# Attention with the keys on the partitions, and three norms centred inside one accumulation group

## The reference

```python
x = _layernorm(x + _L0_attn_ref(x, ...))   # two mamba directions, norms, a small MLP
x = _layernorm(x + _L0_ffn_ref(x, ...))    # gated FFN, hidden 512, two gelu layers
x = _layernorm(x + _L1_attn_ref(x, ...))   # 8 heads, 2 key heads, causal
x = _layernorm(x + _L1_ffn_ref(x, ...))    # 8 experts, top 2
```

```python
k_lat = (x @ wk_down)   # 2 key heads of 32 latent channels
v_lat = (x @ wv_down)
scores = einsum('bqhrd,bkhd->bhrqk', q, k) * scale, causal mask
probs = softmax(scores, axis=-1)
y = einsum('bhrqk,bkhd->bqhrd', probs, v) @ wo
```

## Time and profile before

| | |
|---|---|
| time, 3 runs | 2446.17 us median (2445.69 to 2449.73) |
| the profiled execution | 2451.41 us |
| its span, first to last instruction | 2449.6 us |
| mean granted TensorE clock | 0.863 |

### The profile page before, as it was taken

How to read it: one execution, slowest core, us unless ns; L and a number is a source line. 1 busy time by engine, 2 the same in 40 slices (tenths; PEclk the granted TensorE clock), 3 DMA queues, 4 the chain that set the end, 5 groups by cost and what they waited for, 6 DMA issues and landing times.

```text
span 2449.6 us, 28585 instructions
## 1 busy us (share of the span) xinstructions
PE 1828.0 (75%) x7192; PEld 829.5 (34%) x7192; DVE 1663.3 (68%) x2756; ACT 1221.4 (50%) x2140; POOL 956.7 (39%) x870
## 2 busy tenths in 40 slices
PE   5424976788768887788777887688867788667788
PEld 2201333343324333343333433343333433333344
DVE  2996478845789378873788557884687927887143
ACT  3333655546445465536555365554644456553252
POOL 0453146422455035450464324642354604544031
PEclk9556988899889997799887998889977999889998
DMA  7984465606555274543756156560755536453000
GB/s 200 222 218 112 106 161 146 168 14 177 135 145 134 62 175 130 134 100 86 172 146 146 45 132 154 133 171 25 183 134 129 130 78 163 130 144 75 0 1 5
DMA packets 102732, 301.56 MB, mean 123 GB/s; under 512 B 15216, under 2 KB 31232, under 8 KB 102528
## 3 DMA queue, kind: packets, MB, share of 16 engines
q1 hardware_dynamic: 98304, 297.20, 48.5%
q10 hardware_dynamic: 4224, 2.10, 0.3%
HBM read 280.39 MB, written 18.87 MB: 122 GB/s over the span
## 4 chain that ended last, share of the span: by engine, by line
issue 43%; PE 24%; DVE 17%; POOL 10%; ACT 4%; DVEq 1%; POOLq 0%; SPq 0%; DMA 0%; ACTq 0%
PE ps_g L626 10%; DVE sb_hst L1107 7%; POOL sb_hc L1322 6%; PE ps_g L703 3%; DVE ps_in L1100 3%; POOL sb_h L1336 2%; PE ps_g L711 2%; PE ps_att L626 2%; PE ps_y L579 2%; PE ps_att L723 2%; DVE sb_nmax L1218 1%; POOL sb_res L1348 1%; ACT sb_mix L948 1%; POOL sb_dd L1312 1%; DVE sb_h L1268 1%
## 5 line engine op out<-in xcount | busy, mean ns | idle before, releaser
L1322 POOL TENSOR_TENSOR sb_hc<-sb_hst,sb_crep 128x512 f32<-128x512 f32 x512 | 652.5, 1275 | 637.9 <-DVE sb_hst L1107 637.9
L1107 DVE TENSOR_TENSOR_SCAN sb_hst<-sb_ring,ps_in 128x512 f32<-128x512 f32 x512 | 620.9, 1213 | 16.1 <-ACT sb_ring L854 16.1
L854 ACT ACTIVATE sb_ring<-sb_ring,sb_A 128x512 f32<-128x512 f32 x512 | 349.6, 714 | 82.6 <-DMA sb_ring<-spread_dram 81.8
L1100 DVE TENSOR_TENSOR ps_in<-sb_ring,ps_brow 128x512 f32<-128x512 f32 x512 | 351.8, 687 | 11.8 <-DMA sb_ring<-spread_dram 3.6
L703 PE MATMUL ps_g<-sb_g,sb_qz 128*128 128x512 f32 (+3 forms) x512 | 243.7, 565 | 93.2 <-DVE sb_qz L1209 92.5
L579 PE MATMUL ps_y<-sb_hc,sb_const 128*32 128x512 f32 x1024 | 173.4, 757 | 158.0 <-POOL sb_hc L1322 153.6
L940 ACT ACTIVATE sb_h<-ps_g,sb_nmax 128x128 f32<-128x128 f32 (+3 forms) x256 | 135.0, 528 | 299.9 <-DVE sb_nmax L1218 289.8
L1336 POOL TENSOR_TENSOR sb_h<-sb_h,sb_rz 128x128 f32<-128x128 f32 (+3 forms) x256 | 191.1, 748 | 207.3 <-DVE sb_rz L1222 203.1
L1312 POOL TENSOR_TENSOR sb_dd<-sb_dd,sb_texp 128x512 f32<-128x512 f32 x32 | 40.8, 1274 | 588.7 <-ACT sb_dd L817 588.7
L711 PE MATMUL ps_g<-sb_const,sb_h 128*128 128x128 f32 x640 | 144.6, 332 | 139.1 <-POOL sb_h L1336 116.4
L791 ACT ACT_TABLE_LOAD x162 | 207.8, 1283 | 3.6 <-PEq L1379 0.8
(11 more groups left out here) (220 smaller groups left out, 2778.0 us busy)
## 6 DMA issues: line engine op xcount, KB each, us to landing
sb_ring<-spread_dram SPq DMA_DIRECT2D x512, 512.0 KB, 5.3
spread_dram<-sb_dd SPq DMA_DIRECT2D x32, 512.0 KB, 5.6
sb_xtok<-in_L_attn_x_dram SPq DMA_DIRECT2D x8, 256.0 KB, 6.1
sb_ew<-in_L_ffn_w_dram SPq DMA_DIRECT2D x2, 1024.0 KB, 7.3
out_dram<-sb_lnv ACTq DMA_DIRECT2D x8, 256.0 KB, 2.5
sb_h<-in_L_ffn_h_w_dram SPq DMA_DIRECT2D x1, 1024.0 KB, 8.4
sb_g<-in_L_ffn_h_w_dram SPq DMA_DIRECT2D x1, 1024.0 KB, 9.1
sb_ew<-in_L_ffn_w_dram SPq DMA_DIRECT2D x8, 128.0 KB, 5.4
```

The lines of the kernel that those rows point to most:

```text
L854: act.activation(ring[:, n % RING, 0, :], ring[:, n % RING, 0, :], ACT.Exp, scale=A[d][:, g:g + 1]).then_inc(sem["dA"], 1)
L1100: dve.tensor_tensor(ps_in[n % 2][:], ring[:, n % RING, 1, :], ps_brow[:], ALU.mult).then_inc(sem["dbu"], 1)
L1107: dve.tensor_tensor_scan(hst[:, n % 3, :], ring[:, n % RING, 0, :], ps_in[n % 2][:], 0.0, ALU.mult, ALU.add).then_inc(sem["scan"], 1)
L1322: pool.tensor_tensor(hc[:, n % 6, :], hst[:, n % 3, :], crep[n // NU][:], ALU.mult).then_inc(sem["hc"], 1)
```

## The change

Two parts.

**Norms.** Norms 0, 1 and 3 get their residual inside the accumulation group, already centred: `mo0` and `mo1` are `center @ xkept` plus two products with weights whose mean over channels is taken off before the loop; `mo2` is `fwnc @ s` (centring matrix times the norm weight) plus the two products of the MLP; `mo3` is `center @ xkept` plus `finc @` the scaled norm 2. The biases become `cb`, added as the bias of the square and in the scaling. So `cen0` to `cen3`, both L1159, L1166, L1171, L1177 and L1178 go; the steps `cen` and `ffo`'s separate group go, so that every step after `mo` moves one to three slots earlier and `var` of norms 0 and 1 now comes ahead of the convolution in PE's stream.

**Attention.** Keys sit in a zero-padded tile `kz` (POOL clears 128x2048 once per sequence), one group of 32 rows per key head and half of the query tiles; the queries are computed by 16 narrow products straight into their rows. First 16 steps compute scores with queries on the partitions, only for their maxima (one DVE reduction over two key heads at once). The maxima are split into three bf16 parts and turned by PE in 8 transposes. Then 11 steps in 10 rounds compute the scores again with the keys on the partitions (`turned_scores`, two blocks of 128x512 per round), add the negated maxima by a product with `pick`, take exp of 1024 elements on ACT, and multiply with values and with ones (`values`), so that the sum over keys comes out as a second PSUM result `ps_z`. Ln and Exp on ACT and one product on DVE per key head give `yT`. All copies of the query, the sums, reciprocals, POOL products, turns and PSUM copies of the old form go. `dt_step` selects its activation table explicitly.

With `follow()` and the new `COST`, `var4` lies in slot 24 (before 23), the 16 maxima in 27 to 33, the rounds in 34 to 43 (two of them in 40), `ao` in 44 (before 51), the MoE steps in 46 to 75.

```diff
-C_ID, C_CEN, C_MEAN, C_RED, C_MASK, C_LT, C_END = 0, 128, 256, 384, 512, 640, 704
+C_ID, C_CEN, C_MEAN, C_RED, C_MASK, C_LT, C_PICK, C_END = 0, 128, 256, 384, 512, 640, 704, 708
...
+TILES = ((0, 3), (1, 2))
+MAXIMA = 2 * REP * 2
+def maximum(i):
+    return i // (2 * REP), i // 2 % REP, i % 2
+def rounds():
+    units = [[(t, j) for t in tiles for j in range(t + 1)] for tiles in TILES]
+    return [(k, pair) for k in range(KV) for pair in zip(*units)]
+ROUNDS = rounds()
+LAST = len(ROUNDS) // KV
...
-COST = dict(ln=1.44, ff=1.28, ab=2.2, g=4, q=2.5, att0=0.9, att1=0.62, lg=2, moe=2.75, end=1.21, unit=1.28)
+COST = dict(ln=1.44, ff=1.28, ab=2.2, g=4, q=2.5, s0=0.5, s1=0.25, e=2.0, lg=2, moe=2.75, end=1.21, unit=1.28)
...
+                pe.wait_ge(sem["xkeep"], row("xkeep", 1))
                 pe.wait_ge(sem["gated"], row("gated", 4))
                 for d in range(2):
-                    product(f"mo{d}", [wout[d][:, h, :] for h in range(NH)], [gT[d][:, h, :] for h in range(NH)])
+                    product(f"mo{d}", [center] + [wout[d][:, h, :] for h in range(NH)],
+                            [xkept[:]] + [gT[d][:, h, :] for h in range(NH)])
                 yield
+                for d in range(2):
+                    variance(d, (sq, yy)[d][:])
+                yield
+                pe.wait_ge(sem["s"], row("s", 1))
                 for h in range(2):
+                    product(f"ff{h}", [ffw1[:, h * P:(h + 1) * P]], [nf[:, 0, :]])
+                yield
                 pe.wait_ge(sem["relu"], row("relu", 2))
+                product("mo2", [fwnc[:]] + [ffw2[:, h, :] for h in range(2)], [nf[:, 0, :]] + [hrel[:, h, :] for h in range(2)])
+                yield
+                variance(2, sq[:])
+                yield
+                pe.wait_ge(sem["norm"], row("norm", 3))
+                product("mo3", [center, finc[:]], [xkept[:], nf[:, 1, :]])
+                yield
+                variance(3, sq[:])
...
+                    for k in range(KV):
+                        pe.matmul(ps_pair[i % 2][:, k, 0:(t + 1) * P], qT[:, tl, r, :], kz[:, 2 * k + hf, 0:(t + 1) * P],
+                                  start=True, stop=False)
+                    for k in range(KV):
+                        ins = pe.matmul(ps_pair[i % 2][:, k, t * P:(t + 1) * P], identb[:], maskb[:], start=False, stop=True)
                     done(ins)
+                def turned_scores(i):
+                    k, units = ROUNDS[i]
+                    claim(f"e{i}")
+                    for hf, (t, j) in enumerate(units):
+                        pe.matmul(ps_pair[0][:, hf, :], kz[:, 2 * k + hf, j * P:(j + 1) * P],
+                                  qT[:, TILES[hf].index(t), :, :], start=True, stop=False)
+                    for hf, (t, j) in enumerate(units):
+                        ins = pe.matmul(ps_pair[0][:, hf, :], pick[:, 2 * k + hf, :], mT[:, TILES[hf].index(t), :, :],
+                                        start=False, stop=(j < t))
+                    for hf, (t, j) in enumerate(units):
+                        if j == t:
+                            ins = pe.matmul(ps_pair[0][:, hf, :], maskb[:],
+                                            identb[:].unsqueeze(1).broadcast_to([P, REP, P]), start=False, stop=True)
+                    done(ins)
+                def values(i):
+                    pe.wait_ge(sem["pexp"], row("pexp", i + 1))
+                    for hf, (t, j) in enumerate(units):
+                        for into, w in ((ps_att, vlat[:, j, k * LAT:(k + 1) * LAT]), (ps_z, ones[:])):
+                            for r in range(REP):
+                                ins = pe.matmul(into[LAT * r:LAT * (r + 1), t * P:(t + 1) * P], w,
+                                                pexp[i % 3][:, hf, r * P:(r + 1) * P],
...
+                for i in range(len(ROUNDS) + 1):
+                    if i < len(ROUNDS):
+                        turned_scores(i)
+                    if i >= 1:
+                        values(i - 1)
                     yield
...
+                        act.activation(pexp[i % 3], ps_pair[0][:], ACT.Exp).then_inc(sem["pexp"], 1)
+                    if i in (LAST, 2 * LAST):
+                        act.activation(logz[:], ps_z[:], ACT.Ln).then_inc(sem["logz"], 1)
+                        act.activation(rz[:], logz[:], ACT.Exp, scale=-1.0).then_inc(sem["rz"], 1)
...
+                    dve.tensor_reduce(nmax[:, tl, r, :, hf], ps_pair[i % 2][:, :, 0:(t + 1) * P], AX.X, ALU.max,
+                                      negate=True).then_inc(sem["smax"], 1)
+                    if i % (MAXIMA // 2) == MAXIMA // 2 - 1:
+                        split(tl)
...
+                        dve.tensor_tensor(yT[k], ps_att, rz[:], ALU.mult).then_inc(sem["yT"], 1)
...
+                pool.wait_ge(sem["full"], row("full", R_USE["fo"][2] + 1))
+                pool.memset(kz[:], 0.0).then_inc(sem["kz"], 1)
```

383 lines of the change are left out of this document (191 added, 192 removed).

## The result

The changed kernel takes 2477.01 us (median of 4 runs, 2474.93 to 2477.62), the kernel before in the same session 2447.95 (4 runs, 2445.69 to 2456.29): a ratio of 1.0099, 95% interval 1.0079 to 1.012. It is 1% slower, where 2397 us was forecast, with a range up to 2455. The profiled execution after took 2477.16 us, its span 2475.4, at a granted clock of 0.887.

A forecast was written before the change was run, and what follows sets the result against it. No engine bound throughout: PE and norm round trips at the start, PE in FFN, DVE in attention and MoE. -7.2 - 18.9 + 18 = -8.1 a period, seven times -57, with the rest -49: 2397 us median; likeliest 2375 to 2415, range 2350 to 2455.

The forecast's parts named there:

- the FFN's: FFN stage: one more unit before the q step costs 0, as PE is the bound; without that cover 1.9 us.
- Start, -7.2: Start of the period (convolution, dt, norms): first FFN product after 50.5 us instead of 57.7; -3 to -10 us.
- What lies under the convolution: Start: Ln, Exp, scalings and the sum for the norms run under the convolution, about 6.3 us.
- Attention, -18.9: Attention with q and k: 89.5 us instead of 108.4 a period, with 18 units inside and not 25.
- upper bound for the rounds, 43: Attention: ten rounds and two reduce take 39 us at 3.7 a round, 43 with the upper bounds.
- MoE, +18: MoE: seven more units, a gate and the third dt_step are paid because DVE is full; +18 us, at least +12.
- The last sequence, +4: Last sequence, running alone without units: norms -4 and attention +8 (61.1 to 69), 4 us more.
- The norms' 4 us: Last sequence alone: the norm changes save 4 us.
- The first, rounds at a lower clock: Attention rounds take 4.5 us at a lower clock, +64: 2461 us; deciding from 4.3 a round. Slower outcomes: 0.15.
- The second, gain handed back in MoE in full: Attention's gain returns in MoE, start gains little (-3 a period): 2433, up to 2441 us. Range 2415 to 2451: 0.18.
- The third, DVE as the clock of everything: Whole period follows DVE's loss of 19 us: 2321 us, half-way 2360. Faster than forecast, down to 2321: 0.17.

The follow-up runs named there:

- early_e5: late_e5 with g0 and g1 put two slots earlier (9 and 10) and ab2, ab3 one slot earlier, all else left: 2380.16 us.
- late_e5: Changed kernel with the first g step in slot 11 and a round's assumed cost raised from 2.0 to 5.0: 2298.83 us, ratio 0.9363.
- g_early: Kernel before, only its first steps moved to the change's places (g0, g1 in slots 9, 10), with the table load then needed: 2529.35 us, ratio 1.0314.
- dt_ahead: Changed kernel with the second dt_step moved ahead of the GELU steps, from slots 11 and 12 to 8 and 9: 2463.38 us, ratio 1.0047.
- late_e kernels: Changed kernel with the first g step in slot 11 and a round's assumed cost at 3.0, 4.0 or 5.0: 2368.85, 2330.07 and 2298.83 us.
- norms_only: Kernel before with only the norm half of the change, g0 and g1 in slots 9 and 10: 2456.75 us, ratio 1.0016.
- g_late: Changed kernel with two PREP_FOLLOW entries lowered from 2 to 1, ab steps in slots 7 to 10, first g step in 11: 2454.25 us, ratio 1.0004.
- late_e4: Changed kernel with the first g step in slot 11 and a round's assumed cost raised from 2.0 to 4.0: 2330.07 us, ratio 0.9501.
- norms_late: Kernel before with the norm half of the change, each step from slot 11 on in its old slot: 2370.5 us, ratio 0.9655.
- att_e5: Kernel before with only the attention half of the change and a round's cost at 5.0, fo and ao in their old slots: 2372.12 us, ratio 0.9674.
- g3_in_16: late_e5 with g3 alone moved from slot 15 to 16, behind PE's first reduce: 2341.62 us, ratio 0.9562.
- e4_g3_15: late_e4 with g3 alone moved from slot 16 to 15, ahead of PE's first reduce: 2281.23 us, ratio 0.9312.

## Why the prediction was wrong

**The step that failed** is the FFN's: "One unit more lies before the q step (15 for 14). PE is the bound and DVE has 16 us free: **0**". It counted units and DVE's free time and did not look at the order in ACT's queue. The stage took 9.2 us more a period, about 64 of the 75 us by which the profiled execution (2477.16) missed its forecast (2402). early_e5 against late_e5 moves `g0` and `g1`, with `ab2` and `ab3`, and has 11.4 us in the FFN and 10.4 a period; g_early has 10.8 a period with nothing of the change but places; dt_ahead shows that the wait is bound to the GELU steps and not to `dt_step`. The prediction rested on a stage in which PE was busy for 44.5 of 49.7 us; but PE's own order has `reduce` between the products, and `reduce` depends on ACT, DVE and POOL in turn. DVE's free time was no cover: it was free because it waited. The rest of the miss is MoE and the last sequence, with about 32 and 10 us more than forecast, less about 26 and 3 by which attention and start did better.

**Start, -7.2.** Right: -7.6 in the mean, -7.6 to -9.4 by kernel, with five table loads in it and the roots under the convolution. (What lies under the convolution, put at about 6.3 us, took 4.1, from 1106.38 to 1110.49; its seven instructions of at most 0.69 us add to 4.8.) By the Trainium skill (ScalarE: Activation LUTs, What ACT_TABLE_LOAD costs) a drain stands beside each load. The trace after has none, as the earlier trace rows had none: the load at 1151.91 took 1.28 us and the exp behind it started at 1153.21.

**Attention, -18.9.** -22.6; right in kind. Before the first maximum 13.1 us from `fo`; maxima with seven units, a `gate` and a `dt_step` 33.6 (37 forecast); from turning the maxima to the first exp 6.2; ten exps in 35.0, that is 3.9 a round for 3.7; from the tenth exp to the residual of `ao` 6.3. exp of 1024 elements took 1.02 for 1.11. (The prediction's upper bound for the rounds, 43, does not follow from its own upper prices: 2.92 + 0.16 + 1.37 is 4.45 a round, 46.7 with the two `reduce`.) The reductions took 0.41, 0.69, 0.93 and 1.21 us in the mean, close to what was worked out.

**MoE, +18.** +22.6, for seven units, a `gate` and a `dt_step`; DVE is busy for 81.7 of 91.7, 89%. The mechanism is shown by the late_e kernels (87.2, 78.6, 73.1, 70.4 as `ao` moves from slot 45 to 51, 2.8 us a slot). The term came out a quarter larger: DVE's work in the stage grew by 18.5 us (63.2 to 81.7), near the 17 in the term, and its idle time by 3.8 (6.1 to 9.9), for which the term had 1.

**The last sequence, +4.** +14.4: the mechanism was right, the sizes were not. Its attention went from 69.8 to 82.7 us (+12.9 for +8): the maxima took 23.4 us (20 forecast) and the turn to the first exp 6.2 (4.3 forecast), where the first four products of a round took 3.75 us. The norms' 4 us did not appear; in this stretch the time goes with the granted clock. The stretch from the last norms of the sequence before to the first FFN product, in norms_only and then in g_late, which issue the same instructions in it:

```profile
2241.61:2270.00 28.39, 17.96 (x35) 6.48 (x35) 5.83 (x19) 10.31 (x17) 0.00 (x0) 0.93 0.03 9
```
```profile
2231.82:2267.85 36.03, 25.61 (x35) 8.80 (x35) 5.83 (x19) 10.31 (x17) 0.00 (x0) 0.64 0.03 8
```

The same 35 instructions took 17.96 us of PE at a clock of 0.93 and 25.61 at 0.64. The kernel before had 32.1 us there at 0.86, the change 33.9 at 0.70.

**The rivals.** The first, rounds at a lower clock, is not what happened: the clock in the rounds was 0.94 and a round 3.9 us, under the 4.3 from which it would have decided. Its time (2461) lies nearer than the forecast's, for a reason that is not there. Its page's rule (the Trainium skill, TensorE: Matmul & The Clock Gate, HAM oscillation), that pauses between bursts pull the clock down, finds agreement in the last sequence, at 0.64 to 0.93 with waits of 0.8 to 3.4 us between the norms' products, and in the FFN of late_e4, at 0.65 after PE's wait of 4.30 us. The rounds, where ACT's exp leaves PE pauses of about 1 us at most, kept 0.94. The second, gain handed back in MoE in full, is what the table shows for attention and MoE (-22.6 and +22.6); it had the start's gain small, and that was kept and lost in the FFN. The third, DVE as the clock of everything, fell: DVE gave up 135 us.

**What the forecast should have asked.** It took the slots as given and priced them one stage at a time. The change had two gains, 82 us and 80 us (norms_late and att_e5 against the kernel before of their groups), and a schedule that cost 178: 81 for the place of `g0` and `g1`, with `ab2` and `ab3` a slot early (early_e5), and about 97 for the seven units, the `gate` and the `dt_step` that left the attention, where DVE is idle for half of the rounds, for MoE, where they are paid (early_e5 at 2380, the change at 2477: attention 102.2 to 94.5, MoE 69.9 to 91.7, 14.1 a period). The prediction had seen that DVE would be half idle in the rounds and more than 90% busy in MoE, and did not draw the conclusion that the table of costs, not the code, was then the largest term. That `g3` can cost the same way, by standing behind the `reduce`, g3_in_16 and e4_g3_15 show; in the change it stands ahead of it (slot 14), and there the early `g0` and `g1` hold the scans up. What stays open: why the attention of norms_only and g_early is 1.5 and 2.4 us longer than that of norms_late. Their MoE is 3.0 and 2.6 us longer with `ao` one slot earlier, which fits the 2.8 us a slot of the late_e kernels; but no run moves that step alone. Nor does one tell why the early `g0` and `g1` cost 11.4 us of the FFN in early_e5 and 4.7 in norms_only (48.3 for 43.6 in norms_late).

## What to carry to other kernels

When steps are added to or taken from a hand-made interleaving, list the new order on each in-order engine and look for an instruction that waits for a long producer (here a GELU behind eight products) ahead of short links of another chain; free time on the engines behind it covers nothing. After making a step cheaper, set its weight in the schedule by what it leaves idle, not by its own work: the rounds took 3.9 us, were listed at 2.0, and did best of the weights tried at 4.0 to 5.0, which drew other work into them. Time a change in the old order of everything around it before judging it: both halves here made the kernel over 3% faster, and in the order that came with them they measured 0% and 2% slower.

## What the runs showed that was not expected

- Moving steps by one or two slots changed the time by 3.1% (g_early, with a table load in the code) and 3.5% (early_e5 against late_e5, no other edit).
- The same products took 43% longer at a granted clock of 0.64 than at 0.93 (25.61 and 17.96 us), in a stretch with nothing beside it and with the same instructions; the two kernels differ in what ran before it, and what sets the clock there no run shows. A few us in the last sequence are therefore no measure of a change.
- One wait of PE of 4.3 us in the FFN went with 7 us of time (50.2 to 50.6 for 43.6): the products behind it ran at about 0.66 us each instead of 0.44 (5.27 / 8, 10.56 / 24), at a granted clock of 0.65.
- The FFN took 43.6 us to a tenth in six kernels with different slots: there PE is busy for 41.0 of the 43.6 us, with no wait over 0.9 (late_e5), and the moves of `g1` and `fo` cost nothing at all.
